# A one-head cross-attention that streams its keys through two buffers instead of holding four, two of them loaded ahead

## The chip, the cores and the metric

The kernel runs on one core of one Trainium2 chip. The metric is the device time of one execution in microseconds (us), lower is better. The kernel before takes 2512.89 us (median of 3 runs, 2511.21 to 2517.93).

The engines are named as in the profile: PE (TensorE, matrix products; PEld is its weight load), DVE (VectorE), ACT (ScalarE), POOL (GpSimd) and SP (SyncE). SP does no arithmetic: it issues the DMA transfers from the chip's memory (HBM) into the on-chip buffers, one after the other, and waits on semaphores in between. A wait on SP holds up every transfer written behind it.

## The reference

The program is four layers of a Perceiver-like network on 8 sequences (batches) of 64 tokens of width 256, with a context of 8 x 1601 rows of width 128. Fifteen sub-layers run one after the other, and each adds its result to `x`. The change touches two neighbours, a mixture of experts (`l0f`) and a cross-attention with one head (`l1x`):

```python
def _L0_ffn_ref(x, Wg, W1, W2, W3, Ws1, Ws2, Ws3):        # 8 experts of hidden width 352, top 2, and a shared one of 704
    h = jax.nn.silu(jnp.einsum('tc,ech->eth', xf, W1)) * jnp.einsum('tc,ech->eth', xf, W2)
    y = jnp.einsum('eth,ehc,te->tc', h, W3, w)
    hs = jax.nn.silu(xf @ Ws1) * (xf @ Ws2)
    return y + (hs @ Ws3).reshape(b, t, c)

def _L1_xattn_ref(query, key, value, Wq, bq, Wk, bk, Wv, bv):   # key = value = the context
    q = jnp.einsum('bld,de->ble', query, Wq) + bq
    k = jnp.einsum('bld,de->ble', key, Wk) + bk
    v = jnp.einsum('bld,de->ble', value, Wv) + bv
    attn = jax.nn.softmax(jnp.einsum('bqe,bke->bqk', q, k), axis=-1)
    return jnp.einsum('bqk,bke->bqe', attn, v)

x = x + _L0_ffn_ref(_layernorm(x), ...)
x = x + _L1_xattn_ref(_layernorm(x, axis=-1), ctx_512, ctx_512, ...)
```

## The kernel before, in words

All 512 tokens stay on the core. Each stage is one or more blocks: inside a block every engine runs its own instruction list and they meet through semaphores; at a block's end all engines, SP too, meet at a barrier.

**The expert stage (`experts`, called by `gated_experts("l0f", ...)`).** The shared expert counts as two, so there are ten experts of hidden width 352. For each one SP loads a "guide" (both input projections, 704 KB) into one of two slots of `wg`, and a "down" matrix (384 KB) into one of two slots of `wd`. ACT rounds each to a high part (L1306, L1312), POOL takes the rest as a low part (L1366, L1372), and PE multiplies in three passes (L592 to L594). PE works on expert e while ACT and POOL split the weights of e+1. On ACT the split of the next guide stands ahead of the silu of the current expert's products, so a late guide holds up the current expert too. SP's list begins with guides 0 and 1, down 0, guide 2, down 1, guide 3 and down 2, then (L1220, L1221) calls `fetch_ahead`, and then the loop fetches guide 4, down 3, guide 5, down 4, and so on.

`fetch_ahead` is `first_pairs` here: eight transfers, the context of the attention's pairs 0 and 1. They go to buffers that `one_head_keys` has allocated around both stages.

**The one-head stage (`one_head_cross`).** The 8 batches are handled in 4 pairs; a pair's 2 x 64 queries fill 128 rows. The key projection is folded into the query, so the raw context serves as keys and as values. A pair needs four transfers: for each of its two batches the transposed context (`keysT`, 800.5 KB) and the context by rows (`keys`, 832 KB). Before, four buffer sets are held. Pairs 2 and 3 are fetched at the start of the stage, ahead of the weights of stage `l1a`. Two small dense blocks make the query, and then `one_head_attention` runs. PE's order in it is written out by hand:

```python
scores(0)
for p in range(PAIRS):
    pe.wait_ge(probs_half, p + 1); turn_part(p, 0); turn_part(p, 1)
    if p + 1 < PAIRS:
        scores(p + 1)
    pe.wait_ge(probs_ready, p + 1); turn_part(p, 2); turn_part(p, 3)
    if p: turn_value(p - 1)
    values(p)
```

`scores(p)` (L630) begins with `pe.wait_ge(landed[p], 64)`: all four transfers of its pair, 16 counts each. `turn_part` (L642) transposes the probabilities, `turn_value` (L663) the result, and `values(p)` (L655) multiplies the turned probabilities with `keys` and at its end raises `value_ready`.

Of the kernel before, what the change touches and what calls it, by code (L numbers as in the profile page):

```python
# [24 lines left out]
P = 128  # L25
# [46 lines left out]
class Weights:  # L72
# [8 lines left out]

    def chunks(self, name, n):
        return self(name).rearrange("p (k n) -> p k n", k=n)


OneHeadKeys = namedtuple("OneHeadKeys", "keysT keys landed hold fetch")


ContextKeys = namedtuple("ContextKeys", "cTh cTl ch cl raw fetch_keysT fetch_keys")
# [6 lines left out]
def perceiver_kernel(nc, dram, packs, out):  # L96
    with ExitStack() as stack:
# [3 lines left out]
        def sb(name, shape, dt=F32, where=stack):  # L101
            made_so_far[name] = made_so_far.get(name, 0) + 1
            return where.enter_context(nc.sbuf_tensor(f"{name}_{made_so_far[name]}", shape, dt))
# [25 lines left out]
        def weights(name):  # L129
            return Weights(regions[order.index(name) % 2], packs[name][0])  # L130
# [467 lines left out]
        def keys_in(chunk):  # L598
            return P if chunk < KCH - 1 else KLAST

        def one_head_attention(q, term, keysT, keys, landed):

            PAIRS = B // 2
            names = ("chain", "scores_half", "scores_ready", "top_ready", "probs_half", "probs_ready", "turned_ready",
                     "turned_act", "turned_dve", "value_ready", "value_kept", "value_turned", "value_stored")
            with ExitStack() as own, signals(nc, *names) as \
# [10 lines left out]
                half_cols = slice(0, 2 * BANK), slice(2 * BANK, KEYS)  # L617

                with nc.Block() as block:
                    @block.tensor  # L620
                    def _(pe):
                        def scores(p):
                            pe.wait_ge(landed[p], 64)
                            for n in range(4):
                                if p and n in (0, 2):
                                    pe.wait_ge(probs_ready if n else probs_half, p)
                                w = min(BANK, KEYS - n * BANK)
                                for half in range(2):
                                    rows = slice(half * S, half * S + S)
                                    last = pe.matmul(ps[rows, n, 0:w], q[:, 2 * p * S + half * S:2 * p * S + half * S + S],  # L630
                                                     keysT[p][:, half, n * BANK:n * BANK + w], start=True, stop=True)
                                if n == 1:
                                    last.then_inc(scores_half, 1)
                            last.then_inc(scores_ready, 1)

                        def turn_part(p, g):
                            n = 2 * p + g // 2
                            if n:
                                pe.wait_ge(turned_act if g % 2 else turned_dve, n)
                            for k, chunk in enumerate(PARTS[g]):  # L640
                                w = keys_in(chunk)
                                last = pe.transpose(ps[0:w, 4 + g % 2, k * P:(k + 1) * P],  # L642
                                                    probs[:, p % 2, chunk * P:chunk * P + w], ident[:])
                            last.then_inc(turned_ready, 1)

                        def values(p):
                            if p:
                                pe.wait_ge(value_kept, p)
                            for k in range(KCH):
                                if k % 4 == 0:  # L650
                                    pe.wait_ge(turned_act if (k // 4) % 2 else turned_dve, 2 * p + k // 8 + 1)
                                w = keys_in(k)
                                for half in range(2):
                                    rows = slice(half * S, half * S + S)
                                    last = pe.matmul(ps[rows, 6, 0:CD], probsT[0:w, k, rows], keys[p][0:w, half, k, :],  # L655
                                                     start=(k == 0), stop=(k == KCH - 1))
                            last.then_inc(value_ready, 1)

                        def turn_value(p):
                            pe.wait_ge(value_kept, p + 1)  # L660
                            if p:
                                pe.wait_ge(value_stored, p)
                            pe.transpose(ps[:, 7, 0:P], value[:, p % 2, :], ident[:]).then_inc(value_turned, 1)  # L663

                        scores(0)
                        for p in range(PAIRS):
                            pe.wait_ge(probs_half, p + 1)
                            turn_part(p, 0)
                            turn_part(p, 1)
                            if p + 1 < PAIRS:  # L670
                                scores(p + 1)
                            pe.wait_ge(probs_ready, p + 1)
                            turn_part(p, 2)
                            turn_part(p, 3)
                            if p:
                                turn_value(p - 1)
                            values(p)
                        turn_value(PAIRS - 1)
# [479 lines left out]
                        low(3, last, 1)  # L1158
                        scale_values(c, False)

        def experts(guide, down, count, hidden, combine, bias=False, norm=True, fetch_ahead=None):

# [7 lines left out]
            with ExitStack() as own, signals(nc, *names) as \  # L1172
# [23 lines left out]
                with nc.Block() as block:  # L1196
                    @block.sync
                    def _(sp):
# [18 lines left out]
                        fetch_guide(1, 1, True)  # L1217
                        fetch_down(0, 0, True)
                        two(1, True)
                        if fetch_ahead is not None:  # L1220
                            fetch_ahead(sp)  # L1221
                        with sp.Fori(2, count // 2) as i:
                            two(i)
                        if count % 2:
# [679 lines left out]
                rows_to_norms(token_rows(oT, w.chunks("wo", per), add_to_x, row=w("bo", 1) if row else None),  # L1904
                              [(x, xn, (), None)], [(xT, None, None)])

        @contextmanager
        def one_head_keys():

            names = "pair_landed0", "pair_landed1", "pair_landed2", "pair_landed3"  # L1910
            with ExitStack() as own, signals(nc, *names) as landed:
                keysT, keys = [], []

                def hold(p, where):
                    keysT.append(sb("keysT", [P, 2, KEYS], where=where))
                    keys.append(sb("keys", [P, 2, KCH, CD], where=where))

                def fetch(sp, p):
                    for half in range(2):
                        sp.dma_start(keysT[p][:, half], dram["ctxT"][2 * p + half][:, 0:KEYS]).then_inc(landed[p], 16)  # L1920
                        sp.dma_start(keys[p][:, half], dram["ctx"][2 * p + half].rearrange("p (k d) -> p k d", d=CD))\
                            .then_inc(landed[p], 16)

                hold(0, own)
                hold(1, own)
                yield OneHeadKeys(keysT, keys, landed, hold, fetch)

        def one_head_cross(context):
            weights_here("l1x")
            w = weights("l1x")  # L1930
            with ExitStack() as tmp:
                for p in range(2, B // 2):
                    context.hold(p, tmp)
                    context.fetch(nc.sync, p)
                fetch_next("l1x")
                q = sb("q", [P, N], where=tmp)
                qT = sb("qT", [P, KC, N], where=tmp)
                term = sb("term", [P, B // 2], where=tmp)
                dense(feature_rows(w.chunks("wq", KC), xT, qT, w("bq")))
                wkT = w.chunks("wkT", KC)  # L1940
                bk = w("bk")

                dense([([(wkT[:, k, :], qT[:, k, :]) for k in range(KC)], P, N, "act", copy_to(q[:]))] +
                      [([(qT[:, k, p * P:(p + 1) * P], bk[:, k:k + 1]) for k in range(KC)], P, 1, "dve",
                        copy_to(term[:, p:p + 1])) for p in range(B // 2)])
                one_head_attention(q, term, context.keysT, context.keys, context.landed)
                wv = w("wv").rearrange("p (k n) -> p k n", k=1)
                rows_to_norms(token_rows(q[:].rearrange("p (k n) -> p k n", k=1), wv, add_to_x, row=w("bv", 1)),
                              [(x, xn, (), None)], [(xT, None, None)])
# [239 lines left out]
                                + [(ones[0:1, :], w("bias", 1))], P, D, "dve", add_to_x(t)) for t in range(NT)],  # L2189
                              [(x, xn, (), None)], [(xT, None, None)])  # L2190

        def gated_experts(name, routed, total, hidden, kind, bias=False, fetch_ahead=None):

            weights_here(name)
            fetch_next(name)
# [1 line left out]
            with ExitStack() as own:  # L2197
# [6 lines left out]
                with signals(nc, "chain", "gate_ready") as (chain, gate_ready), nc.Block() as block:  # L2204
# [6 lines left out]
                    def _(dve):  # L2211
# [3 lines left out]
                            link(dve.tensor_copy(shared, std[:].unsqueeze(1).broadcast_to([P, total - routed, NT])))  # L2215
                        else:
                            link(dve.memset(shared, 1.0))
                experts(dram[name + "_guide"], dram[name + "_down"], total, hidden, combine, bias, name != "l3f", fetch_ahead)


        held, inner, mid = two_attentions()
# [2 lines left out]
            inner_attention("l0a", True, True, "bo", lambda t: plus(mid[:, t, :], xn[:, t, :]),  # L2224
                            [(mid, inner, (), (gains("gamma"), gains("beta"))), (x, xn, (inner,), None)])
        plain = [(x, xn, (), None)]
        with one_head_keys() as context:
            def first_pairs(sp):
                context.fetch(sp, 0)
                context.fetch(sp, 1)  # L2230

            gated_experts("l0f", 8, 10, 352, "pair", fetch_ahead=first_pairs)
            one_head_cross(context)
        recurrence()
        capacity_experts()
        many_head_cross("l2x", 64, 64 ** -0.5, True)
# [182 lines left out]
```

## Time and profile before

| | |
|---|---|
| time, median of 3 | 2512.89 us |
| time of the profiled execution | 2512.89 us |
| its span, first to last instruction | 2511.1 us |
| busy: PE, PEld, DVE | 86%, 72%, 59% of the span |
| busy: ACT, POOL | 47%, 19% |
| data moved | 145.33 MB, mean 58 GB/s |
| experts `l0f` | from about 776 to 929 us |
| one-head stage `l1x` | from about 929 to 993 us |

The profile is of the execution whose time stands beside it; 1.8 us of that time lie outside the span. The shares are means over fifteen stages. What the change is worth is read in the two stages of the last two rows, 217 us of the span together.

### The profile page before, as it was taken

The numbers are of one execution on the slowest core, as the hardware profiler recorded it, in microseconds if no ns is written. First come the engines' busy times: TensorE is split into PE (matmuls) and PEld (weight loads), VectorE is DVE, ScalarE is ACT, GpSimd is POOL, SyncE is SP. The second block draws the span as 40 slices with busy tenths as digits, with TensorE's granted clock in tenths as the row PEclk, the third lists the DMA queues.
The fourth block names the chain that finished last, engine by engine and source line by source line (L and its number), as shares of the span: only waits on it lengthen the run. The fifth ranks groups of instructions, "written<-read, shape, count | busy, mean of one in ns | idle before, by whom it ended". The sixth has DMA issues, their size and how long they took to land. (4 is left out here: it accounts for less than half of the span.)

```text
span 2511.1 us, 43499 instructions
## 1 busy us (share of the span) xinstructions
PE 2165.8 (86%) x15168; PEld 1803.1 (72%) x15168; DVE 1489.0 (59%) x3324; ACT 1183.5 (47%) x2411; POOL 469.7 (19%) x381
## 2 busy tenths in 40 slices
PE   3867999999886887259899999986998999999878
PEld 1645999999455764138599999965767999998567
DVE  6445777777234444640477777743346777776346
ACT  1234666766223432211366666632326666665244
POOL 2213222220002320000222221100323222210034
PEclk9788999999977997669999999995999999999779
DMA  4252101000003321025201010001211010100022
GB/s 193 71 206 77 41 28 41 27 27 0 34 10 116 149 98 61 0 93 228 77 28 41 28 40 27 0 1 47 92 70 56 30 39 27 40 14 1 10 65 81
DMA packets 32314, 145.33 MB, mean 58 GB/s; under 512 B 3760, under 2 KB 9136, under 8 KB 28848
## 3 DMA queue, kind: packets, MB, share of 16 engines
q1 hardware_dynamic: 32176, 143.53, 16.0%
q8 instruction: 81, 1.33, 0.2%
q14 instruction: 57, 0.47, 0.1%
HBM read 126.90 MB, written 13.90 MB: 56 GB/s over the span
## 5 line engine op out<-in xcount | busy, mean ns | idle before, releaser
L1095 DVE TENSOR_TENSOR pTl<-ps,pTh 128x512 fp32r<-128x512 f32 (+1 forms) x768 | 438.9, 584 | 110.7 <-ACT pTh L1011 109.8
L1011 ACT ACTIVATE pTh<-ps 128x512 fp32r<-128x512 f32 (+1 forms) x768 | 357.1, 519 | 193.7 <-PE ps L899 183.5
L592 PE MATMUL ps<-pTh,ch 128*128 128x256 f32 (+1 forms) x1248 | 383.3, 307 | 6.2 <-DVE pTl L1095 1.3
L593 PE MATMUL ps<-pTl,ch 128*128 128x256 f32 (+1 forms) x1248 | 348.7, 279 | 0.0
L594 PE MATMUL ps<-pTh,cl 128*128 128x256 f32 (+1 forms) x1248 | 348.3, 279 | 0.0
L592 PE MATMUL ps<-cTh,qh 128*128 128x512 f32 (+2 forms) x768 | 276.2, 360 | 15.2 <-POOL ql L853 8.1
L593 PE MATMUL ps<-cTl,qh 128*128 128x512 f32 (+2 forms) x768 | 268.4, 349 | 0.0
L594 PE MATMUL ps<-cTh,ql 128*128 128x512 f32 (+2 forms) x768 | 268.2, 349 | 0.0
L1082 DVE TENSOR_REDUCE top<-ps 128x1 f32<-128x802 f32 x192 | 189.5, 987 | 115.9 <-PE ps L594 115.9
L592 PEld LDWEIGHTS ps<-pTh,ch 128*128 128x128 f32 (+1 forms) x1248 | 235.1, 188 | 22.3 <-DVE pTl L1095 21.8
L593 PEld LDWEIGHTS ps<-pTl,ch 128*128 128x128 f32 (+1 forms) x1248 | 235.8, 189 | 0.1
L594 PEld LDWEIGHTS ps<-pTh,cl 128*128 128x128 f32 (+1 forms) x1248 | 234.6, 188 | 0.0
L1084 DVE TENSOR_REDUCE top<-ps 128x1 f32<-128x799 f32 x192 | 189.0, 984 | 14.2 <-PE ps L594 4.2
L899 PE MATMUL ps<-ident,probs 128*128 128x128 f32 (+1 forms) x1248 | 184.6, 274 | 13.2 <-DVE pTl L1095 11.5
L1000 ACT ACTIVATE normed<-ps,ntop 128x802 f32<-128x802 f32 x192 | 177.0, 930 | 33.4 <-DVE ntop L1087 33.1
L899 PE MATMUL ps<-ident,normed 128*128 128x128 f32 (+1 forms) x1248 | 183.7, 273 | 1.4 <-DVE pTl L1095 1.4
L1000 ACT ACTIVATE probs<-ps,ntop 128x802 f32<-128x802 f32 x192 | 177.0, 938 | 0.0
L592 PEld LDWEIGHTS ps<-cTh,qh 128*128 128x128 f32 x768 | 146.0, 190 | 36.0 <-POOL ql L853 10.5
L899 PEld LDWEIGHTS ps<-ident,probs 128*128 128x128 f32 (+1 forms) x1248 | 145.2, 140 | 22.8 <-DVE pTl L1095 13.6
L593 PEld LDWEIGHTS ps<-cTl,qh 128*128 128x128 f32 x768 | 147.1, 192 | 17.1
L594 PEld LDWEIGHTS ps<-cTh,ql 128*128 128x128 f32 x768 | 146.6, 191 | 16.9
L592 PE MATMUL ps<-xh,wgh 128*128 128x512 f32 (+1 forms) x280 | 114.9, 410 | 48.9 <-POOL wgl L1366 42.2
(327 smaller groups left out, 3957.4 us busy)
## 6 DMA issues: line engine op xcount, KB each, us to landing
w<-l1f_w_in SPq DMA_DIRECT2D x16, 1024.0 KB, 6.1
raw<-ctxT_in SPq DMA_DIRECT2D x16, 801.0 KB, 4.3
raw<-ctx_in SPq DMA_DIRECT2D x14, 832.0 KB, 4.5
wg<-l0f_guide_in SPq DMA_DIRECT2D x10, 704.0 KB, 5.5
z<-ctx_in SPq DMA_DIRECT2D x8, 832.0 KB, 12.8
z<-z SPq DMA_DIRECT2D x8, 832.0 KB, 11.5
keys<-ctx_in SPq DMA_DIRECT2D x8, 832.0 KB, 10.5
zT<-zT SPq DMA_DIRECT2D x8, 801.0 KB, 14.5
```

The source lines that it names most:

```text
L592: pe.matmul(out, high, moving_high, start=start, stop=False)
L593: pe.matmul(out, high, moving_low, start=False, stop=False)
L594: return pe.matmul(out, low, moving_high, start=False, stop=stop)
L899: last = pe.transpose(ps[0:w, turned_bank[slot][g], k * P:(k + 1) * P], probs[slot][:, chunk * P:chunk * P + w], ident[:])
L1000: nc.scalar.activation(probs[slot][:, cols], flat[:, cols], ACT.Exp, bias=ntop[:, slot:slot + 1], scale=scale, accum_out=total[:, slot, ha ...
L1011: nc.scalar.activation(pTh[0:w, PARTS[g][0]:PARTS[g][0] + n, slot, :], ps[0:w, turned_bank[slot][g], 0:n * P].rearrange("p (k r) -> p k r" ...
L1082: dve.tensor_reduce(top[:, slot, 0:1], flat[:, half_cols[0]], AX.X, ALU.max).then_inc(top_step, 1)
L1084: dve.tensor_reduce(top[:, slot, 1:2], flat[:, half_cols[1]], AX.X, ALU.max)\
L1095: dve.tensor_tensor(pTl[0:w, at, slot, :], ps[0:w, turned_bank[slot][g], 0:n * P].rearrange("p (k r) -> p k r", r=P), pTh[0:w, at, slot, : ...
```

## The change

The buffers of four pairs (`keysT`, `keys`, one tensor each per pair) become two tensors `cT` and `c` with two slots each, allocated inside the one-head stage. Pair p uses slot p % 2. Nothing of the attention is fetched in the expert stage any more: pairs 0 and 1 are fetched at the start of the one-head stage, where pairs 2 and 3 were fetched before, and ahead of the weights of `l1a` as those were. The attention block gets instructions on SP: pair 2 is fetched when `value_ready` reaches 1, pair 3 when it reaches 2. The four landing semaphores become two, and PE waits for 64 x (p // 2 + 1). The arithmetic is the same.

```diff
@@ one_head_attention
-                            pe.wait_ge(landed[p], 64)
+                            pe.wait_ge(landed[p % HELD], 64 * (p // HELD + 1))
...
-                                                     keysT[p][:, half, n * BANK:n * BANK + w], start=True, stop=True)
+                                                     cT[:, p % HELD, half, n * BANK:n * BANK + w], start=True, stop=True)
...
-                                    last = pe.matmul(ps[rows, 6, 0:CD], probsT[0:w, k, rows], keys[p][0:w, half, k, :],
+                                    last = pe.matmul(ps[rows, 6, 0:CD], probsT[0:w, k, rows], c[0:w, p % HELD, half, k, :],
...
+            PAIRS, HELD = B // 2, 2
...
+                    @block.sync
+                    def _(sp):
+                        for p in range(HELD, PAIRS):
+                            sp.wait_ge(value_ready, p - HELD + 1)
+                            fetch(sp, p)
@@ experts
-                        if fetch_ahead is not None:
-                            fetch_ahead(sp)
@@ one_head_cross
-                for p in range(2, B // 2):
-                    context.hold(p, tmp)
-                    context.fetch(nc.sync, p)
+            with ExitStack() as tmp, signals(nc, "pair_landed0", "pair_landed1") as landed:
+                cT = sb("cT", [P, 2, 2, KEYS], where=tmp)
+                c = sb("c", [P, 2, 2, KCH, CD], where=tmp)
...
+                        sp.dma_start(cT[:, p % 2, half], dram["ctxT"][2 * p + half][:, 0:KEYS]).then_inc(landed[p % 2], 16)
+                        sp.dma_start(c[:, p % 2, half], dram["ctx"][2 * p + half].rearrange("p (k d) -> p k d", d=CD))\
+                            .then_inc(landed[p % 2], 16)
+
+                fetch(nc.sync, 0)
+                fetch(nc.sync, 1)
@@ the calls
-            def first_pairs(sp):
-                context.fetch(sp, 0)
-                context.fetch(sp, 1)
-
-            gated_experts("l0f", 8, 10, 352, "pair", fetch_ahead=first_pairs)
-            one_head_cross(context)
+        gated_experts("l0f", 8, 10, 352, "pair")
+        one_head_cross()
```

The instruction lists of PE, DVE, ACT and POOL keep their order. Only SP's changes, at two places. The first is in the expert stage. SP's rows there before, from behind down 2 to the loop's first guide (a semaphore can be printed under the name of an earlier owner: `turned_ready_of3` is `guide_low` here):

```order
L1920 DMA keysT_1<-ctxT_in 128x1601
L1921 DMA keys_1<-ctx_in 128x1664
L1920 DMA keysT_1<-ctxT_in 128x1601
L1921 DMA keys_1<-ctx_in 128x1664
L1920 DMA keysT_2<-ctxT_in 128x1601
L1921 DMA keys_2<-ctx_in 128x1664
L1920 DMA keysT_2<-ctxT_in 128x1601
L1921 DMA keys_2<-ctx_in 128x1664
L1222 UNCONDITIONAL_BRANCH
L1222 ISA
L1202 ISA [waits turned_ready_of3]
L1202 DMA wg_1<-l0f_guide_in 128x1408
```

and now, from down 2 itself on (`chain_of3` is `down_ready`):

```order
L1211 DMA wd_1<-l0f_down_in 128x768 [waits chain_of3]
L1223 UNCONDITIONAL_BRANCH
L1223 ISA
L1205 ISA [waits guide_low_of25]
L1205 DMA wg_1<-l0f_guide_in 128x1408
```

The eight transfers are gone, and guide 4 stands directly behind down 2.

The second place is the one-head stage. SP's rows before, from the dense blocks to the end of the attention block (the ISA rows are semaphores being cleared behind a barrier):

```order
L54 ISA [waits barrier_Pool_Activation_PE_DVE_SP_release]
L54 ISA x2
L54 ISA [waits barrier_Pool_Activation_PE_DVE_SP_release]
L54 ISA x12
L54 ISA [waits barrier_Pool_Activation_PE_DVE_SP_release]
```

and now (`chain_of7` is `value_ready`):

```order
L54 ISA x2
L617 UNCONDITIONAL_BRANCH
L1917 DMA cT_1<-ctxT_in 128x1601 [waits chain_of7]
L1918 DMA c_1<-ctx_in 128x1664
L1917 DMA cT_1<-ctxT_in 128x1601
L1918 DMA c_1<-ctx_in 128x1664
L1917 DMA cT_1<-ctxT_in 128x1601 [waits chain_of7]
L1918 DMA c_1<-ctx_in 128x1664
L1917 DMA cT_1<-ctxT_in 128x1601
L1918 DMA c_1<-ctx_in 128x1664
L616 UNCONDITIONAL_BRANCH
L54 ISA [waits barrier_Pool_Activation_PE_DVE_SP_release]
```

Between the barrier at which the attention block opens and the one that closes it, SP now waits twice and issues four transfers after each wait.

## Rows read from the trace of the kernel before

**Rows 1.** Timeline, SP, expert stage: start us, us, engine, line, operation, out<-in.
```profile
807.60 0.33 SPq L1208 DMA_DIRECT2D wd<-l0f_down_in  x1
807.97 0.43 SPq L1920 DMA_DIRECT2D keysT<-ctxT_in  x1
...
811.39 0.53 SPq L1921 DMA_DIRECT2D keys<-ctx_in  x1
812.27 0.34 SPq L1202 DMA_DIRECT2D wg<-l0f_guide_in  x1
```

**Rows 2.** DMA view, guide transfers issued at 812.27 and 842.50: size, us to landing.
```profile
wg<-l0f_guide_in SPq DMA_DIRECT2D x1, 704.0 KB, 17.4
...
wg<-l0f_guide_in SPq DMA_DIRECT2D x1, 704.0 KB, 5.6
```

**Rows 3.** Waits, 776 to 929 us: total us, times, longest us.
```profile
ACT wgh L1306 <- DMA wg<-l0f_guide_in: 14.2, 2, 10.9
```

**Rows 4.** Timeline, POOL, expert stage; in brackets idle before, and its releaser.
```profile
818.82 1.84 POOL L1372 TENSOR_TENSOR wdl<-wd,wdh 128x768 fp32r<-128x768 f32 x1 [7.64 <-ACT wdh L1312]
...
840.01 1.85 POOL L1372 TENSOR_TENSOR wdl<-wd,wdh 128x768 fp32r<-128x768 f32 x1 [5.69 <-ACT wdh L1312]
...
852.69 1.86 POOL L1372 TENSOR_TENSOR wdl<-wd,wdh 128x768 fp32r<-128x768 f32 x1 [7.64 <-ACT wdh L1312]
```

**Rows 5.** Timeline, PE, one-head stage.
```profile
929.06 6.65 PE L266 MATMUL ps<-normed,weights 128*128 128x512 f32 x8 [0.99 <-PEq L1196]
...
940.89 4.61 PE L630 MATMUL ps<-keysT,q 128*64 128x512 f32 x16 [0.51 <-PEq L244]
...
949.73 4.06 PE L630 MATMUL ps<-keysT,q 128*64 128x512 f32 x16
...
957.57 0.44 PE L655 MATMUL ps<-keys,probsT 65*64 65x128 f32 x4 [0.31 <-ACT probsT L696]
...
958.96 2.92 PE L630 MATMUL ps<-keysT,q 128*64 128x512 f32 x16
...
965.65 0.44 PE L655 MATMUL ps<-keys,probsT 65*64 65x128 f32 x4 [0.19 <-ACT probsT L696]
...
967.04 2.92 PE L630 MATMUL ps<-keysT,q 128*64 128x512 f32 x16
```

**Rows 6.** Timeline, SP, start of the one-head stage.
```profile
930.00 0.34 SPq L1920 DMA_DIRECT2D keysT<-ctxT_in  x1
...
931.33 0.64 SPq L1921 DMA_DIRECT2D keys<-ctx_in  x1
...
933.52 0.45 SPq L1921 DMA_DIRECT2D keys<-ctx_in  x1
```

**Rows 7.** DMA view, keys transfers issued at 931.33 and 933.52.
```profile
keys<-ctx_in SPq DMA_DIRECT2D x1, 832.0 KB, 8.9
...
keys<-ctx_in SPq DMA_DIRECT2D x1, 832.0 KB, 15.3
```

**Rows 8.** Stretches: us; PE, PEld, DVE, ACT, POOL busy; PEclk, DMA, GB/s.
```profile
932.00:934.00 2.00, 2.00 (x3) 0.78 (x3) 0.75 (x1) 0.00 (x0) 0.00 (x0) 0.50 1.02 417
934.00:936.00 2.00, 1.71 (x3) 0.33 (x1) 0.00 (x0) 0.26 (x1) 0.00 (x0) 0.74 0.99 410
936.00:938.00 2.00, 1.26 (x3) 0.68 (x4) 0.00 (x0) 0.43 (x1) 0.00 (x0) 1.00 1.04 433
```

**Rows 9.** Timeline, PE, expert stage.
```profile
825.42 0.39 PE L594 MATMUL ps<-xh,wgl 128*128 128x512 f32 x1
832.49 0.74 PE L592 MATMUL ps<-xh,wgh 128*96 128x512 f32 x1 [6.68 <-DVE gated L1406]
```

**Rows 10.** Stretches, after the wait in the expert stage.
```profile
835.00:836.00 1.00, 1.00 (x3) 0.58 (x3) 0.00 (x0) 0.00 (x0) 0.00 (x0) 0.50 0.00 0
836.00:837.00 1.00, 1.00 (x6) 0.73 (x5) 0.00 (x0) 0.00 (x0) 0.00 (x0) 0.98 0.00 0
```

**Rows 11.** Page, part 6: KB each, median us to landing.
```profile
raw<-ctxT_in SPq DMA_DIRECT2D x16, 801.0 KB, 4.3
```

More of the change, by code:

```diff
@@ L83, in chunks @@
         return self(name).rearrange("p (k n) -> p k n", k=n)
-OneHeadKeys = namedtuple("OneHeadKeys", "keysT keys landed hold fetch")
 ContextKeys = namedtuple("ContextKeys", "cTh cTl ch cl raw fetch_keysT fetch_keys")
@@ L599, in keys_in, with one_head_attention @@
             return P if chunk < KCH - 1 else KLAST
-        def one_head_attention(q, term, keysT, keys, landed):
-            PAIRS = B // 2
+        def one_head_attention(q, term, cT, c, landed, fetch):
+            PAIRS, HELD = B // 2, 2
             names = ("chain", "scores_half", "scores_ready", "top_ready", "probs_half", "probs_ready", "turned_ready",
@@ L1159, in _, with experts @@
                         scale_values(c, False)
-        def experts(guide, down, count, hidden, combine, bias=False, norm=True, fetch_ahead=None):
+        def experts(guide, down, count, hidden, combine, bias=False, norm=True):
             chunks = -(-hidden // P)
@@ L1905, in many_head_cross, with one_head_cross @@
                               [(x, xn, (), None)], [(xT, None, None)])
[L1907 to L1916, printed above, removed]
+        def one_head_cross():
+            weights_here("l1x")
+            w = weights("l1x")
+            with ExitStack() as tmp, signals(nc, "pair_landed0", "pair_landed1") as landed:
+                cT = sb("cT", [P, 2, 2, KEYS], where=tmp)
+                c = sb("c", [P, 2, 2, KCH, CD], where=tmp)
                 def fetch(sp, p):
                     for half in range(2):
[L1920 to L1931, printed above, removed]
-                for p in range(2, B // 2):
-                    context.hold(p, tmp)
-                    context.fetch(nc.sync, p)
+                        sp.dma_start(cT[:, p % 2, half], dram["ctxT"][2 * p + half][:, 0:KEYS]).then_inc(landed[p % 2], 16)
[3 more added lines that the diff above has]
+                fetch(nc.sync, 1)
                 fetch_next("l1x")
@@ L1945, in one_head_cross @@
                         copy_to(term[:, p:p + 1])) for p in range(B // 2)])
-                one_head_attention(q, term, context.keysT, context.keys, context.landed)
+                one_head_attention(q, term, cT, c, landed, fetch)
                 wv = w("wv").rearrange("p (k n) -> p k n", k=1)
@@ L2190, in capacity_experts, with gated_experts @@
                               [(x, xn, (), None)], [(xT, None, None)])
-        def gated_experts(name, routed, total, hidden, kind, bias=False, fetch_ahead=None):
+        def gated_experts(name, routed, total, hidden, kind, bias=False):
             weights_here(name)
@@ L2217, in _ @@
                             link(dve.memset(shared, 1.0))
-                experts(dram[name + "_guide"], dram[name + "_down"], total, hidden, combine, bias, name != "l3f", fetch_ahead)
+                experts(dram[name + "_guide"], dram[name + "_down"], total, hidden, combine, bias, norm=name != "l3f")
         held, inner, mid = two_attentions()
@@ L2226, in perceiver_kernel @@
         plain = [(x, xn, (), None)]
-        with one_head_keys() as context:
-            def first_pairs(sp):
-                context.fetch(sp, 0)
-                context.fetch(sp, 1)
-            gated_experts("l0f", 8, 10, 352, "pair", fetch_ahead=first_pairs)
-            one_head_cross(context)
+        gated_experts("l0f", 8, 10, 352, "pair")
+        one_head_cross()
         recurrence()
```

## The prediction

> **What bounds the kernel now.** I read the busy shares by slice first: PE is the busiest engine on the whole, but a change to two stages is priced in those two. So I went to the waits of the expert stage, the timeline of SP and POOL there, then the timelines of PE and SP in the one-head stage, the time to landing of single transfers, and last the stretches that show DMA rate and granted clock.
>
> The expert stage is bound by PE, except at one place. POOL splits one down matrix per expert, so its rows are a clock for the stage [rows 4]: the steady distance is 852.69 - 840.01 = 12.68 us, but the one before is 840.01 - 818.82 = 21.19 us. The waits name the cause: ACT waited 10.9 us for a guide transfer [rows 3]. That transfer was written behind the eight context transfers, which SP issued from 807.97 to 811.39 and which delayed its own issue to 812.27 [rows 1]; it took 17.4 us to land, where the same transfer later takes 5.6 [rows 2]. So what was loaded ahead is not free before the change: it stalls one expert.
>
> The one-head stage is bound by PE from its first scores on [rows 5]: between 949.73 and the end of the third pair its idle stretches are 0.2 to 0.3 us. All keys are there in time. What the stage will do when they aren't is told by the four transfers of pair 2, issued from 930.00 on into an empty queue, in the very place where pair 0 goes now [rows 6].
>
> **Part 1, the eight transfers leave the expert stage (a gain).** Guide 4 is issued right behind down 2, at about 808.0, and lands 5.6 us later [rows 2], at 813.6. ACT gets to it only when it has finished the split before POOL's 818.82 [rows 4], some 5 us after that landing. The wait goes, nothing of the stage's DMA is late next (each later guide lands in 5.6 us of a 12.68 us period), and PE becomes the bound of this expert as of the others. Gain: 21.19 - 12.68 = 8.5 us. It contains the half-speed piece after the wait. Bounds: at least 0 (if something else holds that expert), at most 8.5, the whole of what this expert takes beyond the period.
>
> **Part 2, pairs 0 and 1 are fetched at the start of the one-head stage.** SP issues the same eight transfers there as before, so I read the new landings off the old ones. Pair 0 lands where pair 2 did: 931.33 + 8.9 = 940.2, and PE starts its scores at 940.89 [rows 5 to 7]. Pair 1 lands where pair 3 did: 933.52 + 15.3 = 948.8, and PE wants it at 949.73. Both are hidden, by 0.7 and 0.9 us. What hides the first is the dense work from 929.06 on, a good part of it at half clock [rows 5, 8]; if that ran faster, PE would find pair 0 missing and start no earlier than now. I take 0; bounds 0 and +1 (both covers gone by half a microsecond each). The weights of the next stage stay behind those eight transfers, as before.
>
> **Part 3, pairs 2 and 3 wait for their buffers (the loss).** SP waits for the end of values(0), which is 957.57 + 0.44 = 958.01 [rows 5], and issues four transfers into an empty queue. Pair 2's took 931.33 + 8.9 - 930.00 = 10.2 us from first issue to last landing [rows 6, 7]. This agrees with the rate: a pair is 2 x (800.5 + 832) KB = 3.34 MB, 8.0 us at the 417 GB/s with a DMA share of 1.02 [rows 8], and some 2 us until it flows. Meanwhile PE has 0.95 us of work, the two turn parts of pair 1 (958.01 to 958.96). Then it stands: scores(2) waits for 64 counts, and behind it in PE's list are the other turn parts, turn_value(0) and values(1). Stall: 10.2 - 0.95 = 9.3 us.
>
> It happens twice, not once. Pair 3's fetch waits for values(1), which PE runs only after scores(2); so pair 3 can't use the first stall to get ahead. In the rows before, values(1) ends at 966.09 and scores(3) starts at 967.04, again 0.95 us [rows 5]: again 9.3 us. ACT and DVE use the stalls for nothing that PE would later wait for: their idle stretches on the path are the 0.2 to 0.3 us above. I count nothing back.
>
> Bounds for a stall: below, the bytes alone at the best rate of the rows, 433 GB/s, 7.7 us, less 0.95: 6.8 us. Above, 10.2 us and SP's longest issue of these rows once more (0.64), less 0.95: 9.9 us. I take 9.3, the same transfers into the same empty queue.
>
> **Part 4, the clock after each stall.** The wait in the expert stage shows it: PE stood from 825.8 to 832.49, the granted clock was at 0.50 (1.2 GHz) when it came back, and at 0.98 in the slice from 836 [rows 9, 10]. So 3.5 us of work ran at half speed and cost 1.8 us. From 929.06 on the clock was low until about 935.0 (0.74 as the mean of 934 to 936) [rows 5, 8], 6 us, costing 3.0. The same shows in the scores: 2.92 us for the 16 products of pair 2 or 3, but 4.61 and 4.06 for those of pair 0 and 1 [rows 5]. Bounds 0 and 3.0 a stall; I take 1.8, from the row that is nearest in kind, a wait for a DMA amid dense work.
>
> The Trainium skill ("TensorE: Matmul & The Clock Gate", section on HAM oscillation) tells of just this pattern, compute that is shorter than its DMA wait, and prices it at about 1.67 us throttled for each wait, of which half is lost. That rule speaks against the change as the trace does, but for 0.8 us where the row has 1.8; with it the sum would be 2 us smaller.
>
> **The sum.** 2 x (9.3 + 1.8) = 22.2 us lost in the one-head stage, 8.5 gained in the expert stage, 0 at its start: +13.7 us. The profiled execution took 2512.89 us, which is also the median, so 2526.6 us.
>
> The Trainium skill ("DMA: Bandwidth & Descriptors", section Where 436 GB/s comes from) says that loads from HBM are held to about 358 GB/s a core. With it a pair would take 9.3 us instead of 8.0, each stall 1.3 us more, and the sum would be +16.3. The trace doesn't agree: 410 to 433 GB/s in every slice in which the queue is full [rows 8].
>
> **The rivals.**
> - *Low price of the clock.* The clock stays at 2.4 GHz or comes back sooner. For it: how long the low spell lasts differs by 2.5 us between the two rows, and a spell can end sooner still. Against: both rows at hand show 3.5 to 6 us at half speed. At nothing: 2 x 9.3 - 8.5 = +10.1, 2523 us.
> - *High price.* 3.0 us a stall, and later stages, which all start at other moments, meet low spells at worse places: +16 and more, 2529 to 2532 us.
> - *The expert stage gives nothing back.* Guide 4 was issued behind down 2 in any case, and the loop starts there; if that held the expert, only the loss stands: +22.2, 2535 us. Against: the releaser is the DMA, and 17.4 against 5.6 us.
> - *Not slower.* The mechanism: a pair's transfers move side by side and land much sooner than four in a row. For it: one transfer of this size alone lands in 4.3 us [rows 11], with far less than the full rate. If the pair landed in 4.3 us, a stall would be 3.4 us, too short for the clock to fall, and the sum 6.7 - 8.5 = -1.8, 2511 us. It decides below 0.95 + 8.5 / 2 = 5.2 us a pair. Against: the DMA share of 1.0 and 2 us from landing to landing.
>
> **How the numbers follow.** Forecast 0.60, low price 0.15, high price 0.13, nothing back 0.05, not slower 0.07. About 0.3% (7.5 us) is what a measurement can tell from no change. The last rival gives 0.02 faster and 0.05 same; a quarter of the low price, together with a shorter landing, comes under +7.5 (0.04). So faster 0.02, same 0.09, slower 0.89. The range 2520 to 2534 holds the forecast and both prices of the clock with the landing's bounds; it leaves out the third rival and the fourth.
>
> **What would show it.** In the profile after: the split of the down weights on POOL at 12.7 us distances throughout; no long wait of ACT for a guide. SP issues two groups of four in the attention, each right after a pair's values. PE idle 9.3 us ahead of the scores of pairs 2 and 3, with the DMA of the context as releaser, and 0.50 in PEclk right after each; the first scores start as soon after the dense blocks as before. The one-head stage is 22 us longer. I am wrong if the stalls are under 5 us, if there is only one, or if the 21 us gap is still in the expert stage.

## The result, and the profile after

The changed kernel takes 2526.25 us (median of 7 runs, 2524.54 to 2531.20) against 2512.89 us (7 runs, 2507.43 to 2517.93): ratio 1.0055, 95% interval 1.0041 to 1.0070. It is 13.4 us slower where +13.7 was forecast. A second, separate measurement (e10, below) gave 1.0062 (1.0039 to 1.0084).

The three places of the prediction are all in the profile after (the line numbers differ from those before by one to three). SP's transfers (start us, us, engine, line, operation): guide 4 is issued 0.7 us after down 2, and two groups of four stand in the attention, of which the first and the last transfer are shown.

```profile
808.94 0.33 SPq L1211 DMA_DIRECT2D wd<-l0f_down_in  x1
809.62 0.34 SPq L1205 DMA_DIRECT2D wg<-l0f_guide_in  x1
...
950.70 0.33 SPq L1917 DMA_DIRECT2D cT<-ctxT_in  x1
...
952.03 0.63 SPq L1918 DMA_DIRECT2D c<-ctx_in  x1
969.85 0.33 SPq L1917 DMA_DIRECT2D cT<-ctxT_in  x1
...
971.17 0.66 SPq L1918 DMA_DIRECT2D c<-ctx_in  x1
```

POOL's splits of the down weights are 12.67 us apart throughout, against the one distance of 21.19 in [rows 4]:

```profile
820.16 1.85 POOL L1373 TENSOR_TENSOR wdl<-wd,wdh 128x768 fp32r<-128x768 f32 x1 [7.62 <-ACT wdh L1313]
...
832.83 1.85 POOL L1373 TENSOR_TENSOR wdl<-wd,wdh 128x768 fp32r<-128x768 f32 x1 [7.62 <-ACT wdh L1313]
...
845.49 1.86 POOL L1373 TENSOR_TENSOR wdl<-wd,wdh 128x768 fp32r<-128x768 f32 x1 [7.62 <-ACT wdh L1313]
```

PE in the one-head stage (in brackets idle time before the row, and its releaser), against [rows 5]:

```profile
933.60 4.61 PE L633 MATMUL ps<-cT,q 128*64 128x512 f32 x16 [0.62 <-DMA c<-ctx_in]
...
942.84 3.61 PE L633 MATMUL ps<-cT,q 128*64 128x512 f32 x16
...
950.22 0.44 PE L658 MATMUL ps<-c,probsT 65*64 65x128 f32 x4 [0.30 <-ACT probsT L699]
950.59 1.09 PE L645 MATMUL ps<-ident,probs 128*128 128x128 f32 x8
960.95 4.79 PE L633 MATMUL ps<-cT,q 128*64 128x512 f32 x16 [9.26 <-DMA c<-ctx_in]
...
966.47 3.34 PE L658 MATMUL ps<-c,probsT 128*64 128x128 f32 x52
969.74 1.09 PE L645 MATMUL ps<-ident,probs 128*128 128x128 f32 x8
981.23 4.88 PE L633 MATMUL ps<-cT,q 128*64 128x512 f32 x16 [10.40 <-DMA c<-ctx_in]
...
986.85 3.32 PE L658 MATMUL ps<-c,probsT 128*64 128x128 f32 x52
```

Pair 0 lands just as PE comes for it: PE's idle time there is 0.62 us and ends with the DMA, where before it was 0.51 us and ended with the barrier. Pair 1 costs nothing. Before the scores of pair 2 PE stands 9.26 us, before those of pair 3 10.40 us, and each time the scores take 4.8 to 4.9 us instead of 2.92. In the other two profiles of this kernel (e8 and e10, below) the two waits are 9.81 and 10.20 us, and 9.40 and 10.12 us. The waits of PE in this stage (total us, times, longest):

```profile
PE ps L633 <- DMA c<-ctx_in: 20.3, 3, 10.4
```

The last transfer of pair 2 and of pair 3, size and us from issue to landing, against [rows 7]:

```profile
c<-ctx_in SPq DMA_DIRECT2D x1, 832.0 KB, 8.9
...
c<-ctx_in SPq DMA_DIRECT2D x1, 832.0 KB, 10.0
```

And the stretches through the first wait (us; PE, PEld, DVE, ACT, POOL busy; PEclk, DMA share, GB/s), against [rows 8, 10]:

```profile
952.00:954.00 2.00, 0.00 (x0) 0.00 (x0) 0.05 (x1) 0.39 (x1) 0.00 (x0) 1.00 0.90 317
...
956.00:958.00 2.00, 0.00 (x0) 0.00 (x0) 0.00 (x0) 0.00 (x0) 0.00 (x0) 0.50 1.04 435
...
962.00:964.00 2.00, 2.00 (x8) 0.56 (x6) 0.00 (x0) 0.00 (x0) 0.00 (x0) 0.50 0.00 0
964.00:966.00 2.00, 2.00 (x13) 0.86 (x10) 1.33 (x2) 0.00 (x0) 0.00 (x0) 0.81 0.00 0
966.00:968.00 2.00, 2.00 (x33) 1.83 (x33) 1.86 (x7) 0.77 (x1) 0.00 (x0) 1.00 0.00 0
```

While all engines wait the DMA moves up to 435 GB/s; the granted clock falls to 0.50 meanwhile, and it is at 1.00 again only in the last row.

The stages, measured from SP's first guide to PE's first product of the one-head stage, and from there to SP's issue of the weights of `l1f`, which stands behind that stage (all from the timelines, us):

| profile of | experts `l0f` | one-head `l1x` | both | against before |
|---|---|---|---|---|
| the kernel before | 153.4 | 64.8 | 218.2 | |
| before, second profile (e7) | 154.6 | 61.9 | 216.5 | |
| the changed kernel | 146.0 | 87.7 | 233.7 | +16.4 |
| changed, second profile (e8) | 145.7 | 87.7 | 233.4 | +16.0 |
| changed, third profile (e10) | 145.9 | 87.6 | 233.5 | +16.2 |
| e1, ahead and streamed | 153.8 | 85.4 | 239.2 | +21.9 |
| e2, four at the start | 146.1 | 76.7 | 222.8 | +5.4 |
| e3, released apart | 146.0 | 64.4 | 210.4 | -6.9 |
| e4, ahead behind the loop | 145.6 | 64.3 | 209.9 | -7.4 |
| e9, the same again | 145.8 | 64.6 | 210.3 | -7.0 |
| e5, busy wait | 145.7 | 84.0 | 229.7 | +12.4 |
| e6, four, two in the block | 145.6 | 66.1 | 211.7 | -5.7 |

The last column is against 217.3, the mean of the two profiles before. Their one-head stages differ by 2.9 us, and the start of the stage explains it: the first dense products and the scores of pair 0 took 6.65 and 4.61 us in the first profile, 5.30 and 2.92 us in the second. The 2.92 us are at a granted clock of 1.00; in the 4.61 us it was 0.50 from 942 to 945.

One number can't be read without a warning. The profiled execution of the changed kernel took 2535.98 us, 10 us more than the median of its timed runs, and 23.1 more than the profiled execution before. The two stages of the change account for 15.5 us. The stage `l3x`, which the change doesn't touch, is another 10.8 us longer, and `l2a` is 5.5 us shorter (later stages are measured from one issue of the next stage's weights by SP to the following one). In `l3x` PE waits twice for nothing that the profile shows, 7.2 us in all.

```profile
PE ps L902 <- issue: 7.2, 2, 4.0
```

The second profile of the kernel before (e7, below) has two such waits too. They come and go from run to run. So does the length of `l2a`: 65.0 us in the first profile before and in e2, 55.6 in e10, and 58.9 to 59.5 in the others.

### The profile page after: what moved, and what is told of

Same layout as the page of the kernel before. It is cut to its first block and busy times, and to the rows that moved or that the text cites. A ratio compares the mean times of both kernels' runs of the same rounds, so it can differ in the third digit from the quotient of the medians.

```text
span 2534.2 us, 43497 instructions
## 1 busy us (share of the span) xinstructions
PE 2170.3 (86%) x15168; PEld 1805.9 (71%) x15168; DVE 1488.3 (59%) x3324; ACT 1183.8 (47%) x2411; POOL 469.7 (19%) x381
## 5 line engine op out<-in xcount | busy, mean ns | idle before, releaser
L902 PEld LDWEIGHTS ps<-ident,probs 128*128 128x128 f32 (+1 forms) x1248 | 146.1, 141 | 30.3 <-DVE pTl L1098 13.4
L902 PEld LDWEIGHTS ps<-ident,normed 128*128 128x128 f32 (+1 forms) x1248 | 148.8, 141 | 11.1 <-DVE pTl L1098 1.6
```

Of the source, the lines that this page charges most:

```text
L902: last = pe.transpose(ps[0:w, turned_bank[slot][g], k * P:(k + 1) * P], probs[slot][:, chunk * P:chunk * P + w], ident[:])
```

## The experiments

**e1: only the streaming.** Pairs 0 and 1 stay in the expert stage, and pairs 2 and 3 wait for their buffers.

```diff
--- the kernel before
-                for p in range(2, B // 2):
-                    context.hold(p, tmp)
-                    context.fetch(nc.sync, p)
...
+                    @block.sync
+                    def _(sp):
+                        for p in range(HELD, PAIRS):
+                            sp.wait_ge(value_ready, p - HELD + 1)
+                            fetch(sp, p)
...
```

> Half of the change: pairs 0 and 1 are still fetched in the expert stage, but pairs 2 and 3 wait for their buffers. My theory (the loss is all in the two waits of PE for pairs 2 and 3): +23 us against the kernel before (two waits of 9.3 to 10.4 us and two slow restarts of about 1.9 us), and the gap of 21 us between two splits of down weights is still in the expert stage. Rival A (part of the loss is pair 0, which now lands just as PE comes for it): about +20 or less. Rival B (part of it lies elsewhere, in the later stages, where the profile of the changed kernel has PE idle for 7 us with nothing to wait for): the one-head stage shows less than +20 and the rest is behind it.

Measured: 1.0091 (1.0069 to 1.0113), which is +23 us by the ratio, 2533.19 us. The expert stage kept its gap (153.8 us). PE's waits in the two stages:

```profile
PE ps L636 <- DMA keys<-ctx_in: 19.8, 2, 10.3
```

Two waits, 19.8 us in all, and the scores of pair 0 wait for no transfer. The streaming alone costs more than the whole change (+21.9 us against +16.2 in the table), so the change gains on its other side. Rivals A and B fall: the loss has its size without pair 0, and it is in the one-head stage (+22 us there).

**e2: only the other half.** Four buffers, nothing ahead, sixteen transfers at the start of the one-head stage.

```diff
--- the changed kernel
-            PAIRS, HELD = B // 2, 2
+            PAIRS, HELD = B // 2, 4
-                    @block.sync
...
                 fetch(nc.sync, 1)
+                fetch(nc.sync, 2)
+                fetch(nc.sync, 3)
```

> The other half: nothing is fetched in the expert stage, four buffers again, all sixteen transfers at the start of the one-head stage. My theory (the eight transfers ahead of a guide cost the expert stage 8.5 us, and streaming alone costs the rest): 8 us faster than the kernel before, about 2505 us; pair 2 lands some 27 us after the first issue, just ahead of its scores, pair 3 at 35 us. Rival (the gap in the expert stage belongs to the loop's start, or pairs 2 and 3 now land too late behind pairs 0 and 1): same as the kernel before within 3 us.

Measured: 1.0007 (0.9986 to 1.0027), 2511.54 us. The gap in the expert stage is gone (146.1 us), and yet my time was missed by some 7 us: the gain is given back by a wait that I hadn't thought of. SP's rows at the start of the one-head stage, the 11th, 13th and 14th transfer and the weights behind the sixteenth:

```profile
923.15 0.49 SPq L1911 DMA_DIRECT2D cT<-ctxT_in  x1
...
924.52 1.77 SPq L1911 DMA_DIRECT2D cT<-ctxT_in  x1
926.33 1.70 SPq L1912 DMA_DIRECT2D c<-ctx_in  x1
...
931.47 0.46 SPq L132 DMA_DIRECT2D weights<-l1a_in  x1
```

Up to the 12th a transfer takes SP 0.3 to 0.5 us to issue (the 4th and the 12th take 0.8). From the 13th it takes 1.7, not much less than the 2 us that such a transfer would take at the 406 to 429 GB/s which the profile shows from 920 to 932 (my estimate). I read this as a full queue, in which SP advances only as transfers land. SP is done at 931.9. It also has to be at the barrier behind the first dense block, where PE had been waiting. PE's rows:

```profile
932.38 3.75 PE L263 MATMUL ps<-qT,weights 128*128 128x512 f32 x4 [9.61 <-PEq L241]
...
958.79 2.92 PE L627 MATMUL ps<-cT,q 128*64 128x512 f32 x16
```

9.6 us of PE at that barrier, and none at pairs 2 and 3. The wait also left the clock low: the granted clock was 0.50 from 928 to 944, the dense products behind the wait took 3.75 and 3.41 us instead of 1.95 and 1.84, and the first scores 5.48 instead of 4.61, about 4 us more. The rival's sign was right for a reason that was neither of its two.

**e6: e2 mended.** SP issues pairs 2 and 3 inside the attention block, where it is not due at a barrier before the end.

```diff
--- e2
-                fetch(nc.sync, 2)
-                fetch(nc.sync, 3)
@@ one_head_attention
+                    @block.sync
+                    def _(sp):
+                        fetch(sp, 2)
+                        fetch(sp, 3)
```

> Four buffers and nothing fetched in the expert stage, as in the run with sixteen transfers at the start, but SP issues pairs 2 and 3 inside the attention block. That run lost 9.6 us of PE at the barrier behind the first dense block, while SP needed 1.7 us for each transfer from the 13th on. If it is SP's full queue that kept the barrier, the wait goes and the kernel is 8 us faster than the one before, about 2505 us; pairs 2 and 3, issued some 10 us later, land just in time or cost 1 to 2 us. Rival (the two stages can't do without a fetch ahead): no faster than 2511 us.

Measured: 0.9979 (0.9959 to 0.9998), 2504.45 us. PE's scores of pairs 0, 2 and 3:

```profile
933.11 4.61 PE L632 MATMUL ps<-cT,q 128*64 128x512 f32 x16 [0.61 <-DMA c<-ctx_in]
...
952.04 2.92 PE L632 MATMUL ps<-cT,q 128*64 128x512 f32 x16 [0.88 <-DMA c<-ctx_in]
...
960.91 2.92 PE L632 MATMUL ps<-cT,q 128*64 128x512 f32 x16 [0.71 <-DMA c<-ctx_in]
```

The barrier wait is gone, three waits of under 1 us are left, and the stages are 5.7 us shorter than before. So what cost e2 its gain was that SP, still issuing, came late to a barrier.

**e3: two buffers, released one by one.** The transposed context of pair p is free after its scores, some 12 us before its rows are.

```diff
--- the changed kernel
                         for p in range(HELD, PAIRS):
-                            sp.wait_ge(value_ready, p - HELD + 1)
-                            fetch(sp, p)
+                            sp.wait_ge(scores_ready, p - HELD + 1)
+                            fetch[0](sp, p)
+                        for p in range(HELD, PAIRS):
+                            sp.wait_ge(value_ready, p - HELD + 1)
+                            fetch[1](sp, p)
@@ scores, values
-                            pe.wait_ge(landed[p % HELD], 64 * (p // HELD + 1))
+                            pe.wait_ge(landed[p % HELD], 32 * (p // HELD + 1))
+                            pe.wait_ge(landed[2 + p % HELD], 32 * (p // HELD + 1))
...
```

> Two buffers and no fetch ahead, as in the changed kernel, but the transposed context of pair p+2 is fetched as soon as the scores of pair p are done, and the rows of the context when its values are done, each with a landing semaphore of its own. If the stalls come from the 10 us between the end of values(p) and the landing of four transfers, they go: PE finds the transposed context there, and the rows land (two transfers, about 6 us) before values(p+2) wants them. Then the time is that of the kernel before less 8 us, about 2505 us. Rival (the DMA queue is what bounds the one-head stage: 13 MB in 60 us): the stalls shrink but stay, 2510 to 2518 us.

Measured: 0.9966 (0.9948 to 0.9983), 2501.95 us. PE's scores of pairs 2 and 3:

```profile
952.78 2.92 PE L636 MATMUL ps<-cT,q 128*64 128x512 f32 x16
...
960.86 2.92 PE L636 MATMUL ps<-cT,q 128*64 128x512 f32 x16
```

No wait, 2.92 us each, with the same two buffers and the same bytes. So neither the buffers' number nor the queue's rate makes the changed kernel slow, but the moments at which a buffer is given back and at which PE asks for what has landed in it. The edit moves both: `scores` now waits for the transposed context alone, and `values` for the rows. No run has one without the other, so their shares are not shown. The rival (the queue bounds the stage) falls.

**e4 and e9: the kernel before, with the eight transfers behind the loop.**

```diff
--- the kernel before
-                        if fetch_ahead is not None:
-                            fetch_ahead(sp)
                         with sp.Fori(2, count // 2) as i:
                             two(i)
+                        if fetch_ahead is not None:
+                            fetch_ahead(sp)
```

> The kernel before with one edit: the eight transfers are issued behind the expert loop, where only down matrices follow them. If they cost 8.5 us because a guide stands behind them, that comes back: about 2505 us, unless the last down matrix, which then lands late, costs PE a wait (it is needed some 12 us after its issue, and would land some 17 us after: up to 5 us lost, 2510 us). Rival (any burst of 6.5 MB beside the experts slows them, by contention in the buffers' memory): the same 2513 us as before.

Measured: 0.9940 (0.9916 to 0.9963), 2495.51 us from 6 runs. PE's scores of pairs 0, 2 and 3:

```profile
926.95 4.61 PE L630 MATMUL ps<-keysT,q 128*64 128x512 f32 x16 [0.52 <-PEq L244]
...
944.99 2.92 PE L630 MATMUL ps<-keysT,q 128*64 128x512 f32 x16
...
953.07 2.92 PE L630 MATMUL ps<-keysT,q 128*64 128x512 f32 x16
```

The same burst beside the same experts costs nothing when no guide stands behind it, so it isn't contention. The last down matrix, which stands behind the burst here, costs nothing either: ACT's one wait for a down matrix is 1.3 us, as in the changed kernel. The timed gain was twice the 7.4 us of the stages, so I ran it again.

> The kernel before with the eight transfers issued behind the expert loop, once more. Its two stages were 8 us shorter in the profile, while the timed difference was 15 us (0.9916 to 0.9963). If only the expert stage changed and the rest was other stages' variation from run to run, the ratio comes nearer to 0.9965 this time (2504 us against 2513). If the whole 15 us belong to the edit, it repeats at 0.994 or less.

Measured: 0.9967 (0.9950 to 0.9983), 2502.15 us from 12 runs. This is the size of the stages' difference; the first value's excess didn't repeat. e4/e9, e3 and e6 each beat both kernels, e9 and e3 by some 8 us against before; their intervals overlap, and the profile doesn't part them either (-7.0 and -6.9).

**e5: PE kept busy in the wait.**

```diff
--- the changed kernel
+                            if p > HELD:
+                                pe.wait_ge(value_stored, p - HELD)
+                            if p >= HELD:
+                                for _ in range(60):
+                                    pe.transpose(ps[:, 7, 0:P], ident[:], ident[:])
                             pe.wait_ge(landed[p % HELD], 64 * (p // HELD + 1))
```

> The changed kernel, with 60 transposes of the identity (0.14 us each at 2.4 GHz, 8.2 us) put ahead of PE's wait for pair 2 and for pair 3, into a part of PSUM that is free then. They fit into the wait and compute nothing that is used. If the slow restart is the clock's answer to PE's idleness, the scores of pairs 2 and 3 take 2.9 us instead of 4.8 and 4.9, and values(1) and values(2) 2.8 to 3.1 instead of 3.3: about 4 us less than the changed kernel in the one-head stage. Rival (the scores are slow because the DMA has just landed, or the memory is busy): they stay at 4.8 us, and the time stays the changed kernel's, 2526 us.

The transposes took 6.7 us, not 8.2. PE's rows:

```profile
948.52 6.71 PE L630 MATMUL ps<-ident 128*128 128x128 f32 x60
958.18 4.61 PE L638 MATMUL ps<-cT,q 128*64 128x512 f32 x16 [2.95 <-DMA c<-ctx_in]
...
967.70 6.71 PE L630 MATMUL ps<-ident 128*128 128x128 f32 x60
978.11 2.92 PE L638 MATMUL ps<-cT,q 128*64 128x512 f32 x16 [3.69 <-DMA c<-ctx_in]
```

After the second filled wait the scores took 2.92 us, after the first 4.61. Both times the data had just landed, so that doesn't make the scores slow. The granted clock goes with them: it was 1.00 in every microsecond through the second wait and its scores, while at the first it was still 1.00 when PE came back at 958.18 and 0.51, 0.50 and 0.50 in the three microseconds from 959 on. So the clock makes the slow restart. That PE's work prevents it is shown once in two tries: all eight unfilled waits of this kind (the three profiles of the changed kernel and e1) were followed by scores of 4.49 to 4.99 us. How long the idleness that is left may be isn't shown: 2.95 us was followed by the low clock, 3.69 us was not. The one-head stage was 3.7 us shorter than the changed kernel's (84.0 against 87.7); 1.7 us of this lie ahead of the scores of pair 2, mostly in dense products and scores that ran at a higher clock before the first filled wait, and 2.0 behind them. The kernel as a whole was slower, 1.0131 (1.0104 to 1.0158), 2540.10 us from 4 runs. Its profile shows two waits for nothing in `l2x`, where no other profile of this study has one of such length, and `l2x` is 483.4 us long there against 467.7 to 469.7 in the others:

```profile
PE ps L907 <- issue: 4.3, 2, 2.5
```

Whether the 120 added instructions of PE cause them by where the code lies in memory was not tried. The total says nothing on the clock.

**e7 and e8: the same two kernels, profiled again.**

> The kernel before, unchanged, for a second profile. Theory 1 (the 7 us that the changed kernel's profile has in the l3x stage, in two waits of PE for nothing, come and go from run to run): this profile can have them, or other stages that differ by some us from the first profile of the same kernel. Theory 2 (they belong to where the changed program's code lies): none of them here, and the stages agree with the first profile to 2 us.

Measured: 2519.85 us, with PE twice idle in `l3x` for no releaser, 4.04 and 3.26 us:

```profile
2097.73 1.11 PE L899 MATMUL ps<-ident,probs 128*128 128x128 f32 x4 [4.04 <-issue]
...
2204.41 0.72 PE L899 MATMUL ps<-ident,probs 128*128 128x128 f32 x4 [3.26 <-issue]
```

Theory 1 holds: it is the same kernel, and the first profile had neither.

> The changed kernel, unchanged, for a second profile. Theory 1: the two waits of PE in the l3x stage can be gone, and the time is then near 2526 us. Theory 2: both are there again. In either case the one-head stage has its two waits of 9 to 10.5 us, and the splits of the down weights are 12.7 us apart.

Measured: 2526.22 us, one such wait (3.0 us), the one-head stage as long as in the first profile (87.7 us), its two waits 9.81 and 10.20 us, as expected.

**e10: the changed kernel timed again.**

> The changed kernel again, on the same chip as the run beside it. Both profiles of it have the expert stage and the one-head stage together 15 to 16 us longer than the kernel before. My theory: ratio 1.004 to 1.008. If the first ratio of 1.0055 came in part from another chip or from luck with the later stages, it leaves this range.

Measured: 1.0062 (1.0039 to 1.0084), 2525.70 us from 12 runs, in the range expected, though the interval reaches a little beyond both its ends.

## Why the prediction was right

**Part 1, the gain.** 8.5 us were forecast, from one distance between two rows, and that distance is now 12.67 (in the second profile before it was 21.75, so the gap itself varies by half a us). The stage is 8.1 us shorter (154.0 on the mean of two profiles to 145.9 on the mean of three), 7.5 against the first profile alone, in which the opening of the stage ran 1 us quicker: from SP's first guide to the split at 818.82 it is 43.1 us there, to the same split at 820.16 it is 44.1 after. e2, e3 and e6 have the gain too, e1 doesn't, and e4 gets it by moving the eight transfers alone. The step that carried it, that the burst costs by its place ahead of a guide and not by its bytes, is shown.

**Part 2, pairs 0 and 1.** Forecast 0, cost 0.1 us. The cover of 0.7 us for pair 0 is just used up: the first dense products took 0.4 us less than in [rows 5] (6.23 against 6.65 us), and the last transfer landed 0.3 us later (9.2 us behind its issue for 8.9).

**Part 3, the two waits.** Forecast 9.3 twice, measured 9.26 and 10.40. Reading pair 2's landing off the old trace was exact: 10.2 us from first issue to last landing, before and after. Pair 3 took 971.17 + 10.0 - 969.85 = 11.3 us. The second wait is the longer one in all four profiles with these waits (9.47 and 10.34 us in e1, 9.81 and 10.20 in e8, 9.40 and 10.12 in e10), by 0.4 to 1.1 us. Why stays open. That pair 2's wait came out within 0.1 us of the forecast is in part luck, since that wait alone varies from 9.26 to 9.81 us. That the waits come one after the other, since the fetch of pair 3 depends on work behind the wait for pair 2, is as forecast.

**Part 4, the clock.** Forecast 1.8 us each; the scores were longer by 4.79 - 2.92 = 1.9 and by 4.88 - 2.92 = 2.0. The granted clock in the stretches, and e5, show that it is the clock. The Trainium skill's price for such a wait ("TensorE: Matmul & The Clock Gate", section on HAM oscillation: about 1.67 us throttled, half of it lost) is less than half of what these rows show, 0.8 us for 1.9 and 2.0. Its pattern, a restart at the low clock after each DMA wait, is what these rows show, but e5 has one DMA wait, of 3.69 us, without it.

**The sum.** The first timing says +13.4 us (its interval allows 10.3 to 17.6), the second, from the ratio, 2512.9 x 0.0062 = +15.6; forecast was +13.7. That the first comes within 0.3 us of it is luck. In the profiles the two stages are 16.2 us longer than the mean of before, 15.4 longer than the first profile of before, from which the forecast was read. That is 1.7 us more than forecast: 1.1 for pair 3, 0.2 for the clock, 0.1 for pair 0 and 1.0 at the opening of the expert stage, which is no part of the change; less 0.3 for values(1) and values(2), which find all their inputs ready after a wait (3.34 and 3.32 us for 3.48), and 0.4 for the first dense products. The timings can't tell 13.7 from 16.2.

**The rivals.** Not slower (transfers side by side): refuted by the landings, 10.2 us for the four of pair 2. Its step from a stall of 3.4 us to no loss of clock was weak as well. In the same trace PE stands 2.73 us before its turn parts at 948.23, and the granted clock, 1.00 from 946 to 948, is 0.50 from 949 to 952; after the 3.69 us in e5 it stayed at 1.00. Nothing back from the expert stage: refuted by e1 and e4, in which the gap stays with the burst and goes with it. The low price of the clock: refuted by the rows. The high price: not reached in the two stages; later stages do vary by several us from run to run, but for both kernels (over all profiles `l3x` by 14 us and `l2a` by 9).

## What to carry to other kernels

A transfer that is issued early isn't free (here it cost 8 us): look at what stands behind it in its queue, and put it behind the last transfer that someone will soon wait for. With two buffers the length of a stall is the time from the release to the last landing, less the work that the reader still has; release each buffer at its own last reader, and let each reader wait on its own semaphore: here the stall vanished with no more memory (e3). A gain or loss of a few us in a kernel of 2.5 ms is safer read from the lengths of the touched stages in two profiles or more than from the whole time of one. Here the two stages together differed by 1.7 us between the two profiles before and by 0.4 among the three after, while `l3x` alone varied by 14.

## What the runs showed of the hardware that I had not expected

- SP issued the first twelve transfers of 0.8 MB in 0.3 to 0.8 us each, but took 1.7 us for each from the 13th on; through a barrier this held PE for 9.6 us (e2). Where eight were issued and the other eight 6 us later (e6), each of the sixteen took 0.3 to 0.8.
- PE waits of 3.0 to 4.4 us with no releaser, in the same stage, at the same instruction (a transpose in the loop of `l3x`), in some executions and not in others: two in the second profile of the kernel before (4.0 and 3.3) and none in the first, two in the first of the changed kernel (7.2 together), one in the second (3.0), two in the third (8.7 together). They go with more time than they last: from SP's issue of the weights of `l3a` to that of `l3f`, `l3x` is 448 to 450 us long in the profiles with no such wait, 453 to 456 with one and 459 to 463 with two, on the means about 6 us for each. What makes the rest isn't known. The count of packets of the instruction queue on the profile's page goes with them: 81 in every profile without such a wait, 90 in every one with one, 99 in every one with two (11 profiles, e5 apart). The Trainium skill ("Runtime: NRT & Kernel Launch", section Instruction fetch mechanics) says that a taken branch outside the fetched window makes the engine wait for its code; that fits a loop, but doesn't say why the same program shows it in one run and not in the next, and no run here shows that these waits are for code. What decides it stays open.
- 60 transposes of 128 x 128 took 6.7 us (0.11 us each) without a wait between them, against 1.09 us for 8 (0.14 us each) in the attention, both at a granted clock of 1.00 (e5).
